# Two-layer attention and MoE kernel on eight cores: probability tiles transposed by DMA instead of on TensorE, and the heads of the second attention staged

## The reference, cut to what matters

```
def _L1_attn_ref(x, Wq, bq, Wk, bk, Wv, bv, proj):      # 16 heads of 64
    scale = sqrt(64)
    q = einsum('bse,hde->bhsd', x, Wq) + bq ...          # k and v likewise
    scores = einsum('bhsd,bhtd->bhst', q, k) / scale
    scores = where(causal, -inf, scores)
    att = softmax(scores, axis=-1) / scale
    z = einsum('bhst,bhtd->bhsd', att, v).reshape(b, s, h * dh)
    return z @ proj
```

## Time and profile before

| | us |
|---|---|
| median of 7 runs (lowest, highest) | 7755.42 (7752.69, 8074.38) |
| the profiled execution, its own time | 7754.34 |
| its span on the slowest core | 7752.8 |
| spans of the eight cores | 7736.3 to 7752.8 |
| mean granted TensorE clock, each core | 0.761 to 0.763 |

### The profile page before, as it was taken

How to read it: one execution, slowest core, us unless ns; L and a number is a source line. 1 busy time by engine, 2 the same in 40 slices (tenths; PEclk the granted TensorE clock), 3 DMA queues, 4 the chain that set the end, 5 groups by cost and what they waited for, 6 DMA issues and landing times. The chain is left out here.

```text
span 7752.8 us, 67899 instructions; the slowest of 8 cores (7736.3 to 7752.8 us)
## 1 busy us (share of the span) xinstructions
PE 5002.4 (65%) x23786; PEld 2346.0 (30%) x23786; DVE 2291.9 (30%) x4515; ACT 1486.9 (19%) x2461; POOL 174.1 (2%) x318
## 2 busy tenths in 40 slices
PE   2499998644443289999999999984233333333333
PEld 2244434211111234444444444432111111112121
DVE  3233333311222312222222222223333333333332
ACT  2211100011122211111111111101223333333333
POOL 0000000000000000000000000000000000000000
PEclk9999999555665589999999999996555555555555
DMA  1112211022221031211222221010000000000001
GB/s 45 27 33 41 41 20 20 1 46 44 33 33 19 0 56 34 45 37 26 40 45 45 35 45 37 9 30 6 11 11 11 11 0 11 1 11 1 11 0 52
DMA packets 70701, 199.15 MB, mean 26 GB/s; under 512 B 8025, under 2 KB 28762, under 8 KB 60512
## 3 DMA queue, kind: packets, MB, share of 16 engines
q0 software_dynamic: 63136, 177.79, 13.7%
q1 hardware_dynamic: 7232, 17.02, 0.7%
HBM read 364.17 MB, written 8.39 MB: 48 GB/s over the span
## 5 line engine op out<-in xcount | busy, mean ns | idle before, releaser
L1113 PE MATMUL p_gps<-s_xn_fm,s_wgr 128*128 128x512 bf16 x4672 | 1773.8, 380 | 32.6 <-DMA s_wgr<-wg 32.6
L1121 PE MATMUL p_gps<-s_xn_fm,s_wur 128*128 128x512 bf16 x4672 | 1773.6, 380 | 12.6 <-DMA s_wur<-wu 12.6
L1139 PE MATMUL p_yps<-s_wd_sb,s_hfm 128*128 128x512 bf16 x4672 | 1011.6, 379 | 0.2 <-DVE s_x_tm L1147 0.2
L1132 DVE TENSOR_TENSOR s_hfm<-p_gps,s_sil 128x512 bf16<-128x512 f32 x584 | 404.0, 692 | 1656.9 <-ACT s_sil L1130 1656.9
L1130 ACT ACTIVATE s_sil<-p_gps 128x512 f32<-128x512 f32 x584 | 349.2, 598 | 2564.6 <-PE p_gps L1113 2508.1
L1113 PEld LDWEIGHTS p_gps<-s_xn_fm,s_wgr 128*128 128x128 bf16 x4672 | 457.7, 98 | 585.3 <-issue 35.7
L1121 PEld LDWEIGHTS p_gps<-s_xn_fm,s_wur 128*128 128x128 bf16 x4672 | 457.7, 98 | 566.4 <-issue 16.9
L1007 PE MATMUL p_ptp<-s_id_b,s_pbufA 128*128 128x128 bf16 x1088 | 146.4, 304 | 746.0 <-DVE s_pbufA L999 665.8
L1007 PE MATMUL p_ptp<-s_id_b,s_pbufB 128*128 128x128 bf16 x1088 | 146.3, 303 | 743.2 <-DVE s_pbufB L999 662.9
L1139 PEld LDWEIGHTS p_yps<-s_wd_sb,s_hfm 128*128 128x128 bf16 x4672 | 452.6, 98 | 556.1 <-issue 34.0
L1147 DVE SCALAR_TENSOR_TENSOR s_x_tm<-p_yps,s_cw_tm,s_x_tm 128x1024 f32<-128x1024 f32 x256 | 328.7, 1284 | 499.6 <-PE p_yps L1139 499.5
(11 more groups left out here) (191 smaller groups left out, 4046.8 us busy)
## 6 DMA issues: line engine op xcount, KB each, us to landing
s_woring<-woT POOLq DMA_DIRECT2D x128, 256.0 KB, 3.9
s_wgr<-wg POOLq DMA_DIRECT2D x29, 1024.0 KB, 16.4
s_wur<-wu POOLq DMA_DIRECT2D x29, 1024.0 KB, 20.9
s_wd_sb<-wd POOLq DMA_DIRECT2D x10, 2816.0 KB, 20.9
s_prring<-proj POOLq DMA_DIRECT2D x64, 256.0 KB, 3.7
s_wd_sb<-wd POOLq DMA_DIRECT2D x9, 1024.0 KB, 10.5
s_x_tm<-x SPq DMA_DIRECT2D x1, 8192.0 KB, 31.9
out<-s_x_tm SPq DMA_DIRECT2D x1, 8192.0 KB, 22.5
```

Of the source, the lines that this page charges most:

```text
L1113: p.op("tensor", lambda e, dc=dc, ts=ts, lo=lo, rslot=rslot, gp=gp: e.matmul(gp, wgr[:, rslot * 4096 + dc * 512 + lo: rslot * 4096 + dc * ...
L1121: p.op("tensor", lambda e, dc=dc, ts=ts, lo=lo, rslot=rslot, up=up: e.matmul(up, wur[:, rslot * 4096 + dc * 512 + lo: rslot * 4096 + dc * ...
L1132: p.op("vector", lambda e, fc=fc, ts=ts, ssl=ssl, up=up, gb=gb: e.tensor_tensor(hfm[:, fc * T + ts * TSL:fc * T + (ts + 1) * TSL], up, ssl ...
L1139: p.op("tensor", lambda e, fc=fc, half=half, c=c, yb=yb: e.matmul(yps[:, yb * 1024 + half * 512:yb * 1024 + (half + 1) * 512], hfm[:, fc * ...
```

## The change

The loop body of `attn1_pass` is cut into four functions, which are called with an offset between heads, and three operations change.

- `st_pt`: the n transposes of a head are DMA transposes on SyncE's queue, SBUF to SBUF, straight from `pbufA`/`pbufB` to `ptbA`/`ptbB`. All those of even heads use one semaphore, `pt1_0`, and those of odd heads `pt1_1`. TensorE's transposes, the PSUM tile `ptp` and ScalarE's copies out of it are gone.
- `st_soft`: the scaling of the probabilities is on GpSimd instead of VectorE.
- `st_ctx`: each matmul with v now depends on all n blocks of its head's transposed tile, where it depended on its own block.
- The scores of even and odd heads use different banks of `psA` when there are one or two matmuls of scores to a head.
- Step i of a tile does the scores of head i, the softmax of head i-1, the transposes of head i-2, and, where i-2 is odd, the matmuls with v of that pair.
- `Prog.dma` leaves a token `('S', name)` without a value. Who depends on it waits until the semaphore has reached the total of all transfers issued on it so far in the program.

```
@@ Prog.op
+            elif tok[0] == 'S':
+                name = tok[1]
+                val = self.dma_sems[name][1]
+                if smax.get(name, 0) < val:
+                    smax[name] = val
@@ Prog.dma
-        sem[1] += 16
-        val = sem[1]
-        tok_done = ('s', sem_name, val)
+        if transpose:
+            def fn(e, out=out, in_=in_):
+                return e.dma_start_transpose(out, in_)
...
         self.op(qeng, fn, r=r, w=w, record=False)
         self.ops[qeng][-1].incs.append((sem[0], 16))
+        sem[1] += 16
+        tok_done = ('s', sem_name, sem[1])
+        tok_tot = ('S', sem_name)
         for (buf, key) in w:
-            buf.dep[key] = [tok_done, []]
+            buf.dep[key] = [tok_tot, []]
         for (buf, key) in r:
-            buf.dep.setdefault(key, [None, []])[1].append(tok_done)
+            buf.dep.setdefault(key, [None, []])[1].append(tok_tot)
@@ attn1_pass
-            ptp = psum("ptp1", 128, 2048, ph, dt=BF16)
...
-                        bk = kjt % 4
+                    bk = (hb * 2 + kjt) % 4
...
-                    p.op("vector", lambda e, pb=pb, Lq=Lq, hb=hb, qt=qt: e.tensor_scalar(
+                p.op("gpsimd", lambda e, pb=pb, Lq=Lq, hb=hb, qt=qt: e.tensor_scalar(
                         pb[:, 0:Lq], pb[:, 0:Lq], sm_sc[:, hb * 4 + 3:hb * 4 + 4],
                         None, ALU.mult), ...
...
-                    for kc in range(qt + 1):
-                        p.op("tensor", lambda e, kc=kc, slot=slot, pb=pb: e.transpose(
-                                ptp[:, slot * 128:(slot + 1) * 128],
-                                pb[:, kc * 128:(kc + 1) * 128], id_b[:]), ...
-                        if len(seg) == 8 or kc == qt:
-                            p.op("scalar", ... e.copy(ptb[...], ptp[...]), ...
+            def st_pt(qt, h):
+                hb = h % 2
+                pb = pbufA if hb == 0 else pbufB
+                ptb = ptbA if hb == 0 else ptbB
+                for kc in range(qt + 1):
+                    p.dma("sync", ptb[:, kc * 128:(kc + 1) * 128],
+                          pb[:, kc * 128:(kc + 1) * 128], f"pt1_{hb}",
+                          r=[(pb, kc)], w=[(ptb, kc)], transpose=True)
...
-                                     r=[(v_tm, (kc, hh // 2)), (ptg, kc)],
+                             r=[(v_tm, (kc, hh // 2))] + [(ptg, k) for k in range(qt + 1)],
...
+                for i in range(16 + 3):
+                    if i < 16:
+                        st_scores(qt, i, Lq, ntile)
+                    if 0 <= i - 1 < 16:
+                        st_soft(qt, i - 1, Lq, ntile)
+                    if 0 <= i - 2 < 16:
+                        st_pt(qt, i - 2)
+                        if (i - 2) % 2 == 1:
+                            st_ctx(qt, i - 2)
```

More of the change, by code:

```diff
@@ L138, in op, with dma @@
         return tok
-    def dma(self, qeng, out, in_, sem_name=None, r=(), w=()):
+    def dma(self, qeng, out, in_, sem_name=None, r=(), w=(), transpose=False):
         if sem_name is None:
@@ L931, in attn1_pass, with st_scores @@
             psB = psum("psB1", 128, 1024, ph)
-            ptp = psum("ptp1", 128, 2048, ph, dt=BF16)
+            def st_scores(qt, h, Lq, ntile):
+                hb = h % 2
+                oc, prt = h // 2, (h % 2) * 64
+                for kjt in range(ntile):
+                    j0 = kjt * 512
+                    w512 = min(512, Lq - j0)
+                    bk = (hb * 2 + kjt) % 4
+                    p.op("tensor", lambda e, oc=oc, prt=prt, qt=qt, j0=j0, w512=w512, bk=bk: e.matmul(
+                            psA[:, bk * 512:bk * 512 + w512],
+                            q_fm[prt:prt + 64, oc * T + qt * 128:oc * T + (qt + 1) * 128],
+                            k_fm[prt:prt + 64, oc * T + j0:oc * T + j0 + w512],
+                            start=True, stop=True),
+                         r=[(q_fm, (oc, qt * 128 // TS))] +
+                           [(k_fm, (oc, (j0 + jj * 128) // TS)) for jj in range(w512 // 128)],
+                         w=[(psA, bk)])
+                    wdiag = (j0 + w512 == Lq)
+                    ee = "vector" if kjt % 2 == 0 else "scalar"
+                    if wdiag:
+                        if w512 > 128:
+                            p.op(ee, lambda e, hb=hb, j0=j0, w512=w512, bk=bk: (
+                                    e.tensor_copy(sc_sb[:, hb * T + j0:hb * T + j0 + w512 - 128],
+                                                  psA[:, bk * 512:bk * 512 + w512 - 128])
+                                    if hasattr(e, "tensor_copy") else
+                                    e.copy(sc_sb[:, hb * T + j0:hb * T + j0 + w512 - 128],
+                                           psA[:, bk * 512:bk * 512 + w512 - 128])),
+                                 r=[(psA, bk)], w=[(sc_sb, (hb, kjt))])
+                        p.op("vector", lambda e, hb=hb, j0=j0, qt=qt, bk=bk: e.tensor_tensor(
+                                sc_sb[:, hb * T + qt * 128:hb * T + (qt + 1) * 128],
+                                psA[:, bk * 512 + (qt * 128 - j0):bk * 512 + (qt * 128 - j0) + 128],
+                                causal[:], ALU.add),
+                             r=[(psA, bk), (causal, None)], w=[(sc_sb, (hb, kjt, "d"))])
+                    else:
+                        p.op(ee, lambda e, hb=hb, j0=j0, w512=w512, bk=bk: (
+                                e.tensor_copy(sc_sb[:, hb * T + j0:hb * T + j0 + w512],
+                                              psA[:, bk * 512:bk * 512 + w512])
+                                if hasattr(e, "tensor_copy") else
+                                e.copy(sc_sb[:, hb * T + j0:hb * T + j0 + w512],
+                                       psA[:, bk * 512:bk * 512 + w512])),
+                             r=[(psA, bk)], w=[(sc_sb, (hb, kjt))])
@@ new lines, in st_pt, with st_ctx @@
+            def st_pt(qt, h):
+                hb = h % 2
+                pb = pbufA if hb == 0 else pbufB
+                ptb = ptbA if hb == 0 else ptbB
[3 more added lines that the diff above has]
+                          r=[(pb, kc)], w=[(ptb, kc)], transpose=True)
+            def st_ctx(qt, h):
+                for kc in range(qt + 1):
+                    for g in range(2):
+                        hh = h - 1 + g
+                        ptg = ptbA if g == 0 else ptbB
+                        p.op("tensor", lambda e, kc=kc, g=g, hh=hh, ptg=ptg, qt=qt: e.matmul(
+                                psB[(g * 64):(g * 64 + 64), g * 512:g * 512 + 128],
+                                v_tm[:, kc * D + hh * 64:kc * D + (hh + 1) * 64],
+                                ptg[:, kc * 128:(kc + 1) * 128],
+                                start=(kc == 0), stop=(kc == qt),
+                                tile_position=(0, g * 64)),
+                             r=[(v_tm, (kc, hh // 2))] + [(ptg, k) for k in range(qt + 1)],
+                             w=[(psB, g)])
+                oc = h // 2
+                for g in range(2):
+                    p.op("scalar", lambda e, oc=oc, qt=qt, g=g: e.copy(
+                            zfm[g * 64:(g + 1) * 64,
+                                (qt % 2) * 1024 + oc * 128:(qt % 2) * 1024 + (oc + 1) * 128],
+                            psB[g * 64:(g + 1) * 64, g * 512:g * 512 + 128]),
+                         r=[(psB, g)],
+                         w=[(zfm, (qt % 2, oc, g))])
```

132 lines of the change are left out of this document (31 added, 101 removed).

## The result

The changed kernel takes 10746.93 us (median of 4 runs, 10742.34 to 10751.49), the kernel before 7755.48 us (10 runs). The ratio is 1.3859, 95% interval 1.384 to 1.3878: slower, by 2991 us. The profiled execution took 10750.86 us with a span of 10749.3 us.

What follows compares the result with a forecast made beforehand. A chain, not an engine, was taken to bound the second attention. Round trips 4843, issue 51, matmuls 223, filling 109, projections 187 and first tile 20 us make 5433 instead of 2437: 10,750 us, range 9,300 to 13,400.

Steps and rivals of the forecast that it cites:

- Each transpose waits for the one ahead of it: On SyncE's queue, the token without a value makes each block of a head wait for the previous landing: 2018 round trips.
- L = 2.4 from the 32 KB load: Round trip of one DMA transpose, 2.4 us, from the 2.3 us gate-weight load plus 0.1 us to the next instruction.
- Rival B: DMA transpose slower than a plain load of its size, L over 3.0 us; at 3.7, 13,375 us in all; chance 0.17.
- rival C: SBUF to SBUF transpose quicker, L between 0.95 and 1.9 us; at 1.3, 8531 us in all; chance 0.12.
- 0.4 us of issue: SyncE's time to issue one transpose between the heads of a pair, 0.4 us, 128 times: 51 us.
- rival A: Waits do not hold SyncE's queue for a round trip; 0.4 us a block, 7009 us in all; chance 0.02.
- break-even of 0.91 us a block: Cost per transposed block on SyncE at which the stage would take its former time: 1846 us over 2018.
- Matmuls with v: On TensorE, no longer beside anything since SyncE waits for them: 159 us plus 64 for hops and latency, 223 us.
- GpSimd covered: GpSimd's scaling, taken as 2.0 us, lies beside the transposes; up to some 25 us for the longest row before it shows.
- Rival D: GpSimd's scaling takes the bound, over 2.4 us for each block of 128 columns; over 11,000 us; chance 0.02.
- The work taken off TensorE and ScalarE brings nothing: The 586 us of transposes and copies removed in the stage gain nothing, as both engines wait for SyncE.
- The signs: Expected in the trace: transposes 2.2 to 2.6 us apart, SyncE's own-DMA waits some 4,800 us, last tile 620 us.

Runs made afterwards that it cites:

- e1: The changed kernel with all transposes of a head waiting only for their semaphore's total before that head: 8800 us, ratio 1.1353 to the kernel before.
- e2: The changed kernel with all blocks of a head in one DMA transpose, 256 instead of 2176: 7299 us, ratio 0.9419 to the kernel before.
- e5: The changed kernel with transposes back on TensorE, copies on ScalarE and scaling on VectorE: 7201 us, ratio 0.9292 to the kernel before.
- e8: The changed kernel with one DMA transpose a head, scaling on VectorE and matmuls with v one step later: 6891 us, ratio 0.889.

## Why the prediction was right, step by step

The forecast was 10,750 us. Direction and mechanism held. That the number came out within 4 us is luck: errors of 100 us and more cancel in the sum, and the stage, 10 us shorter than forecast, began 11 us later than on the core that was profiled before. The chain's pieces of the stage, added up by kind, against the terms:

| term | predicted, us | measured, us |
|---|---|---|
| round trips | 2018 x 2.4 = 4843 | 2012 landings of 2.26 in the mean, 4545; with 0.07 of hops, 4686 |
| issue between the heads of a pair | 51 | 159 |
| matmuls with v and their hops | 223 | 133 + 18 = 151 |
| projections | 187 | 102 + 66 + 13 = 181 |
| filling, and the first tile | 129 | the rest, 246 |
| stage | 5433 | 5423 |

- *Each transpose waits for the one ahead of it.* Right: 1890 waits of SyncE for its own DMA, 2.25 us from start to start in even heads and 2.34 in odd ones, and 1947 us back when e1 takes the wait away.
- *L = 2.4 from the 32 KB load.* Nearly right, by 0.07. The gate weights' row was the right one to take: it and the transposes both land after 2.2 to 2.3 us in the trace after, though one reads HBM and the other transposes. Rival B and rival C, a slower or much faster transpose, are out. e2 shows that most of the price is fixed: 4.38 us for sixteen times the bytes. The fixed 2.0 us that the Trainium skill names (DMA: Bandwidth & Descriptors, "Anatomy of one DMA") lies near the 2.2 measured, but the section's heading gives it for DMAs that GpSimd issues, which the prediction did not say; these are SyncE's.
- *0.4 us of issue.* Wrong: a DMA transpose holds SyncE for 1.09 us, not the 0.40 us of a plain DMA of the same size. It cost only 108 us here, but it would have spoilt rival A: without the waits I priced the kernel at 7009 us, and e1 took 8800. The break-even of 0.91 us a block was sound, and the issue alone lies over it, so that no removal of waits could have made transposes issued block by block on SyncE faster than before.
- *Matmuls with v.* Too high by 72 us, the hop and latency of each pair taken too large.
- *GpSimd covered.* Right in kind. In the fills its 5.45 us for the longest row, not 2.0, cost more than allowed: 58 us of the chain are GpSimd's. Rival D is out: it is busy for 807 of 5435 us.
- *The work taken off TensorE and ScalarE brings nothing.* Right here; e5 and e2 show what it and the staging are worth once no chain of round trips lies over them.
- The 1309 ns that the Trainium skill gives for a transpose by DMA (VectorE: DVE Perf Modes, "The three transpose paths") fits no waited transpose here; the nearest is the 1.27 us from one issue to the next in e1.
- *The signs.* The spacing within a head, the exp and the matmuls with v waiting for DMA, and a DMA share of 9% came as named, and the last tile took 616 us against 620. Three did not: the odd head's first transpose follows by 1.09 us and not 0.4; SyncE's waits for its own DMA sum to 2193 us and not 4,800, as the issue is half of each round trip; and VectorE is busy for 704 us and not 742. None of them changes the path.

The 18 landings of 3.0 to 5.5 us on the chain have company in the trace. Eight of them, 4.0 to 5.5 us, are those beside the first two weight pieces of each of the eight output projections, as the 5.46 us one:

```profile
10632.93 1.12 POOL L157 DMA_DIRECT2D s_prring<-proj  x2
10633.14 8.88 SPq L154 DMA_TRANSPOSE s_ptbA<-s_pbufA  x3
```

Each of the other ten, 3.0 to 3.9 us, had a packet of the instruction queues beside it. Of 80 landings under 2.4 us, picked at random, only three had either. No run moves these transfers, so the cause is likely but not shown.

## What to carry to other kernels

A dependency token that means "all that was issued on this semaphore so far" turns a loop of independent transfers into a chain of round trips when the loop's own transfers are in the total; look in the order of the issuing queue for a wait on the semaphore that the instruction ahead raises. Price a chain of DMAs by the landing of the nearest row and its count, and price its removal by the issue time of that very kind of instruction, which a plain DMA's did not give here. Where many small transposes are wanted, try them in one DMA before arguing over waits: here that gave 3448 us, taking away the waits 1947.

## What the runs showed that I had not expected

- A DMA transpose of 128x128 holds SyncE for 1.09 us alone and 1.23 us with others in flight; one of sixteen blocks holds it for 1.5 to 2.1 us. In the last tiles of e8 (ns, min/median/max):

```profile
L154 SPq DMA_TRANSPOSE s_ptbA<-s_pbufA x9: 1610/1885/2094, 6701.9 to 6829.4; - x9
L154 SPq DMA_TRANSPOSE s_ptbB<-s_pbufB x9: 1518/1592/2027, 6707.7 to 6835.4; - x9
...
DMA to landing us min/median/max: 4.1/4.3/4.4
```

- GpSimd needs 5.45 us for a bf16 row of 2048 columns times a scalar, VectorE 0.75: seven times.
- In the changed kernel cores 0, 2, 4 and 6 span 10733.8 to 10749.3 us and cores 1, 3, 5 and 7 10684.4 to 10693.1. Core 1's transposes hold its queue for 1.079 us where core 2's take 1.095. On the chain the difference is in the landings of odd heads: 1073 of them sum to 2384 us on core 1 (2.21 us in the median) and 2451 us on core 2 (2.27); those of even heads are 16 us longer on core 1. No run separates the cause.
